# Rows of a group of four taken with a step of 4 instead of a step of 2

## The chip, the cores and the metric

The kernel is one program on one core of a Trainium2 chip. The metric is the time of one execution on the device in microseconds (us). The kernel before took 3278.6 us in the median of three runs (3276.79 to 3288.68 us). Its profile was taken of the run of 3288.68 us.

## The reference, cut to what matters

The network is two layers over eight sequences of 512 tokens with 128 features, each sublayer followed by a layer norm: attention, a feed-forward net, a second attention, and a mixture of experts. The change lies in the second attention. For each of 16 heads (64 wide) it computes:

```
q, k, v = x @ Wq, x @ Wk, x @ Wv            # k, v get 4 learned memory rows in front
dots = (l2norm(q) @ l2norm(k).T) * 10
dots = einsum('hg,bgij->bhij', W_pre_th, dots)     # the heads are mixed
dots = where(causal, dots, -max)                   # token i sees the memory and tokens 0..i
dots = where(dots < 64th largest of the row, -max, dots)
attn = einsum('hg,bgij->bhij', W_post_th, softmax(dots))   # mixed again
out  = (attn @ v) * head_scale * sigmoid(x @ Wg + bg);  out @ Wo
```

Each query row is mixed, cut to its 64 largest scores and normed by itself, so which rows are handled together is free.

## The kernel before, in words

The program has three phases: attention and feed-forward net of the first layer, the second attention, and the experts. The second (`second_phase`, line 703, with its body in `second_attention`) takes some 1.9 ms of the span.

**Tiles and units.** A sequence of 512 queries is cut into four tiles of 128 (`TILE_ORDER` = 3, 1, 2, 0). Scores of a tile are written head by head into `dots` (the profile calls it arena), with the query on the partition. Mixing heads needs heads on the partition, so a tile is worked in 16 units of 8 query rows by 16 heads = 128 partitions. One DMA on SyncE's queue (L909) gathers a unit from 8 partitions of `dots` into one of four `mixin` slots. Four units form a group of 32 rows (`GROUP`): all units of a group have the same width, up to the last column that any row of the group sees (`width`). Two units form a pair, and a step works on one pair; a sequence has 32 steps.

**Which rows.** `every(u)` (L833) says which 8 rows of a tile are unit u: a slice of 16 rows with a step of 2. So the first two units of a group share its first 16 rows, and the other two its last 16. The same function places a unit's 8 columns when the weights are turned back: ScalarE's copy into `at2` (L1261) writes 8 columns for each head and key block, 2 apart.

**The steps of a unit.** PE mixes (L1070) and adds a mask (L1072); ScalarE copies the result to `xs` (L1235); VectorE takes the maximum and moments; GpSimd and ScalarE (L1242, twice) find a threshold near the 64th score; VectorE picks the bound from it and writes the chosen weights with their sum (L1354 to L1394); GpSimd scales the second mixing matrix by the sum (L938); PE multiplies the weights with it, which turns them at the same time (`post`, L1083); ScalarE copies them to `at2` (L1261); and once a block of 64 queries is complete, PE multiplies it with the values (`values`, L1116).

**The tail.** Four memory rows stand in front of the keys, so the last 4 columns of a tile (tokens 124 to 127 of its own block) lie beyond its last full key block. `has_tail(s)` is true for a step whose rows can see them: before, only the last of a tile's 8 steps. There PE makes one more small product for each unit (`post_tail`, L1092, 4 columns as weights), ScalarE copies it to `tail` (L1266), and `values` adds its product (L1121) to the last 16 columns of the block.

**Order.** Every engine's order is written out by hand: a table of `put` calls (L788 to L805) lays the other work of the sequence (norms, keys, queries, scores, gates) into three slots A, B and C of each step. PSUM is four pairs of banks. Scores, keys, queries, gates and tails all go through the pair `banks_a` in one order of turns (`A_KEYS`, L862 to L869); PE may fill a bank when the copy two turns before has been read. VectorE and GpSimd wait for the tail's product before they write over the weights that it reads (L1389, L935).

Of the kernel before, what the change touches and what calls it, by code (L numbers as in the profile page):

```python
# [14 lines left out]
P = 128  # L15
# [5 lines left out]
UNSEEN = -2.0 ** 66  # L21
# [20 lines left out]
H1, HD1, MEM, TOPK = 16, 64, 4, 64  # L42
# [3 lines left out]
R8 = P // H1  # L46
SUBS = S // R8
PER_TILE = P // R8
GROUP = 4
RB = 64  # L50
# [4 lines left out]
SEQ = [PER_TILE * t + u for t in TILE_ORDER for half in ((0, 1) if t else (1, 0)) for u in range(PER_BLOCK * half, PER_BLOCK * (half + 1))]  # L55
PAIR = 2
# [20 lines left out]
def width(n):  # L77

    return MEM + GROUP * R8 * (n // GROUP + 1)
# [63 lines left out]
def scope(nc):  # L143

    ctx, sems = ExitStack(), []

    def sb(name, shape, dt=F32):
        return ctx.enter_context(nc.sbuf_tensor(name, shape, dt))

    def sem(name):  # L150
        s = ctx.enter_context(nc.semaphore(name))
        sems.append(s)
        return s

    return ctx, sb, sem, sems
# [547 lines left out]
def second_phase(nc, psum, d, x2_d, x3_d, dots, wts, x2_0):  # L703

    ctx, sb, sem, sems = scope(nc)
    with ctx:
# [7 lines left out]
        vx = sb("vx", [P, TT + 1, H1 * HD1])  # L714
# [1 line left out]
        sq = krow  # L716
        ssq, nrm = sb("ssq", [P, 2 * TT * H1]), sb("nrm", [P, 2, 2 * TT * H1])
        at2 = sb("at2", [P, TT, H1, RB])
        tail = sb("tail", [P, H1, PAIR * R8])
        gate, og = sb("gate", [P, NC, P]), sb("og", [P, NC, P])  # L720
        res = sb("res2", [P, TT, D])
        stats, mv, rstd = sb("stats2", [P, 6]), sb("mv2", [P, 2]), sb("rstd2", [P, 1])
# [52 lines left out]
        def second_attention(block, nb, first, full):  # L775
# [45 lines left out]
            def unit(m):  # L821
                return m // SUBS, SEQ[m % SUBS]

            def pair_of(s):
                return [(z, PAIR * s + z, SEQ[(PAIR * s + z) % SUBS]) for z in range(PAIR)]
# [5 lines left out]
                return m % SUBS // PER_TILE  # L831

            def every(u):  # L833
                at = PAIR * R8 * (u // PAIR)
                return slice(at + u % PAIR, at + PAIR * R8, PAIR)

            def last_piece(n):
                return len(pieces(width(n))) - 1
# [3 lines left out]
                return k < A_SLOTS or SEQ[k] // PER_TILE != SEQ[k - A_SLOTS] // PER_TILE or width(SEQ[k]) < width(SEQ[k - A_SLOTS])  # L842

            def has_tail(s):
                return SEQ[PAIR * s % SUBS] % PER_TILE == PER_TILE - PAIR

            def banks_of(what):
                if what[0] in ("xT", "g"):
# [131 lines left out]
            def _(pe):  # L980
# [6 lines left out]
                def d_bank(key):  # L987
                    if DV.nth(key) > 2:
                        pe.wait_ge(d_free, DV.nth(key) - 2)
                    return banks_d[DV.bank(key)]  # L990
# [105 lines left out]
                def values(r, second):  # L1096

                    b, n = unit(PER_BLOCK * r)
                    t, odd = divmod(n // PER_BLOCK, 2)
                    if second:  # L1100
                        bank = banks_d[DV.bank(("av", r))]
                    else:
                        pe.wait_ge(t_free, T.nth(PER_BLOCK * r + PER_BLOCK - 1))
                        if odd:
                            pe.wait_ge(a_free, A.nth(("tail", STEPS_BLOCK * (r + 1) - 1)))
                            pe.wait_ge(a_free, A.nth(("vx", b, TT, 1)))
                        if r % BLOCKS == 0:
                            pe.wait_ge(a_free, A.nth(("vx", b, TT - 1, 1)))
                            pe.wait_ge(memv_in, 16 * (b + 1))
                        bank = d_bank(("av", r))  # L1110
                    for c in range(NC // 2 * second, NC // 2 * (second + 1)):
                        col = RB * c
                        for k in range(t + 1):
                            for h in (2 * c, 2 * c + 1):
                                at = HD1 * (h % 2)
                                ins = nc.tensor.matmul(bank[at:at + HD1, col:col + RB], vx[:, k, HD1 * h:HD1 * h + HD1], at2[:, k, h, :],  # L1116
                                                       start=k == 0, stop=k == t and not odd)
                        if odd:
                            for h in (2 * c, 2 * c + 1):
                                at = HD1 * (h % 2)  # L1120
                                ins = nc.tensor.matmul(bank[at:at + HD1, col + RB - PAIR * R8:col + RB], vx[:, t + 1, HD1 * h:HD1 * h + HD1],  # L1121
                                                       tail[:, h, :], start=False, stop=True)
                    if second:
                        ins.then_inc(d_full, 1)
# [35 lines left out]
            def _(act):  # L1160

                def filled(key):
                    act.wait_ge(a_full, A.nth(key))
                    return banks_a[A.bank(key)]
# [89 lines left out]
                def posted(s):  # L1254
                    r = s // STEPS_BLOCK
                    if s % STEPS_BLOCK == 0 and r:
                        act.wait_ge(d_full, DV.nth(("av", r - 1)))
                    for z, m, n in pair_of(s):
                        t, u = n // PER_TILE, n % PER_BLOCK
                        act.wait_ge(t_full, T.nth(m))  # L1260
                        nc.scalar.copy(at2[:, 0:t + 1, :, every(u)],  # L1261
                                       banks_t[T.bank(m)][:, 0:P * (t + 1)].rearrange("p (k h i) -> p k h i", k=t + 1, h=H1)).then_inc(t_free, 1)
                    if has_tail(s):
                        bank = filled(("tail", s))
                        for z, m, n in pair_of(s):
                            ins = nc.scalar.copy(tail[0:MEM, :, every(n % PAIR)],  # L1266
                                                 bank[0:MEM, P * z:P * z + P].rearrange("p (h i) -> p h i", h=H1))
                        ins.then_inc(a_free, 1)

# [579 lines left out]
def network(nc, d, x2_d, x3_d, parts_d, maxes_d, gates_d, out_d):  # L1849
    with ExitStack() as ctx:  # L1850
        psum = {k: [ctx.enter_context(nc.psum_tensor(f"p{k}{i}", [P, 512], F32)) for i in range(2)] for k in "aomt"}
        arena = ctx.enter_context(nc.sbuf_tensor("arena", [P, SCORES_N], F32))
        wts2 = ctx.enter_context(nc.sbuf_tensor("wts2", [P, W2_N], F32))
        x2_0 = ctx.enter_context(nc.sbuf_tensor("x2s0", [P, TT, D], F32))
        first_phase(nc, psum, d, x2_d, parts_d, maxes_d, arena, wts2, x2_0)
        second_phase(nc, psum, d, x2_d, x3_d, arena, wts2, x2_0)
        third_phase(nc, psum, d, x3_d, gates_d, out_d, arena)


def constants():  # L1860

    f = np.float32
    half = HD0 // 2
    inv = (1.0 / f(10000.0) ** (np.arange(half, dtype=f) / f(half))).astype(f)
    freqs = np.arange(S, dtype=f)[:, None] * inv[None, :]
    d = np.arange(P) % HD0
    cos, sin = np.cos(freqs)[:, d % half].T, np.sin(freqs)[:, d % half].T
    sin = np.where((d < half)[:, None], -sin, sin)
    q = np.arange(P)
    sums = q[:, None] == q[None, :] // SUM_COLS * SUM_COLS + HD0 + q[None, :] % HD0  # L1870
    heads = (q[:, None] // HD1 == q[None, :] // HD1)
    dpre = (q[:, None] // H1 == q[None, :] // H1)
    dpost = (q[:, None] // H1 == q[None, :] % R8)
    rank = np.broadcast_to((TOPK - 1 - np.arange(WINDOW)) * TAKEN, (P, WINDOW))
    mask_s = np.where(q[None, :] > q[:, None], LOW, 0.0)
    mix = [np.where(np.arange(GROUP * R8)[None, :] > PAIR * (R8 * (v // PAIR) + q[:, None] // H1) + v % PAIR, UNSEEN, 0.0) for v in range(GROUP)]
    return dict(first=[cos, sin, np.eye(P), sums], masks=[np.eye(P), mask_s, mask_s.T],
                second=[np.eye(P), *thresholds(), rank], mix=[np.eye(P)] + mix, heads=heads, dpre=dpre, dpost=dpost,
                ident=np.eye(P))


def thresholds():


    first, slope = np.zeros((P, SUBS), np.float32), np.zeros((P, SUBS), np.float32)

    def quantile(share):

        lo, hi = -10.0, 10.0
        for _ in range(60):  # L1890
            mid = (lo + hi) / 2
            lo, hi = (mid, hi) if (1 + erf(mid / sqrt(2))) / 2 < share else (lo, mid)
        return lo

    for n in range(NARROW_FROM, SUBS):
        for q in range(P):
            seen = PAIR * R8 * (n // PAIR) + PAIR * (q // H1) + n % PAIR + 1 + MEM
            first[q, n] = quantile(1 - (AIM + 0.5) / seen)
            slope[q, n] = -1 / (2 * seen * exp(-first[q, n] ** 2 / 2) / sqrt(2 * pi))
        summed = sqrt(width(n) - GROUP * R8)  # L1900
        first[:, n], slope[:, n] = first[:, n] / summed, slope[:, n] / summed
    return first, slope


def laid_out(a):
# [3 lines left out]
    wq, wk, wv = qkv[:D], qkv[D:2 * D], qkv[2 * D:]  # L1909
    swap = (np.arange(D) // HD0) * HD0 + (np.arange(D) + HD0 // 2) % HD0  # L1910
    c = constants()

    def cols(v):
# [48 lines left out]
```

## Time and profile before

| | |
|---|---|
| median of 3 runs | 3278.6 us |
| the profiled execution | 3288.68 us |
| its span from the first to the last instruction | 3286.9 us |
| mean granted clock of TensorE | 0.911 |
| PE, VectorE, ScalarE, GpSimd busy | 2715.9, 2309.8, 2086.8, 1239.6 us |
| transfers from `arena` to `mixin` | 512, of 18 to 258 KB |
| copies into `at2` | 512, 198.4 us |
| copies into `tail` | 64, 13.2 us |

An engine's busy time says how much work it has, not whether it sets the end: for that the stretches and the waits are read. Steps are 32 to a sequence, and the pattern of one sequence returns eight times.

### The profile page before, as it was taken

To read this page: it belongs to the slowest core of one execution; us is meant where nothing else is said; L and a number is where in the kernel's file an instruction comes from. 1 tells how busy PE (TensorE), PEld (TensorE's weight loads), DVE (VectorE), ACT (ScalarE), POOL (GpSimd) and SP (SyncE) were. 2 spreads that over 40 slices of the span, in tenths; PEclk is the share of its full clock that TensorE was granted. 3 is DMA by queue.
4 is the path that set the end of the run, shared out by engine and by line. 5 is a ranking of instruction groups with operands and counts; after the bars stand their busy time and mean duration, and the time that the engine had idled before them with its cause. 6 is when DMAs were issued, how large, how long until landed. Compare 5 with 4: busy or idle time off the path is not lost. (4 is left out here: it accounts for less than half of the span.)

```text
span 3286.9 us, 59887 instructions
## 1 busy us (share of the span) xinstructions
PE 2715.9 (83%) x18884; PEld 1634.5 (50%) x18884; DVE 2309.8 (70%) x7740; ACT 2086.8 (63%) x5457; POOL 1239.6 (38%) x3658
## 2 busy tenths in 40 slices
PE   3678888888888888888888888888888888876898
PEld 1234333333333456555555555556556556555565
DVE  3445355444423399899799799899799888887465
ACT  0244655555453588788788788787787787874331
POOL 2111011101000256555565565565565565674000
PEclk6678889989889799999899999999999999987899
DMA  2111011001010211211211211211211211221342
GB/s 91 34 36 37 8 37 40 23 19 40 5 45 10 46 32 37 54 33 36 52 37 32 53 39 31 57 36 28 60 37 25 59 39 24 57 47 40 92 98 65
DMA packets 111295, 137.13 MB, mean 42 GB/s; under 512 B 20448, under 2 KB 90592, under 8 KB 110464
## 3 DMA queue, kind: packets, MB, share of 16 engines
q1 hardware_dynamic: 110976, 133.25, 17.8%
q8 instruction: 155, 2.54, 0.3%
q14 instruction: 164, 1.34, 0.1%
HBM read 47.62 MB, written 13.24 MB: 19 GB/s over the span
## 5 line engine op out<-in xcount | busy, mean ns | idle before, releaser
L1242 ACT ACTIVATE junk<-xs,thr 128x420 bf16<-128x420 f32 (+12 forms) x832 | 466.0, 570 | 74.8 <-POOL thr L957 59.8
L1083 PE MATMUL pt<-wsc,attn 128*128 128x128 f32 x2560 | 364.1, 292 | 101.9 <-POOL wsc L938 65.4
L1070 PE MATMUL pm<-mixin,pre_b 128*128 128x258 f32 (+15 forms) x1088 | 371.2, 457 | 91.2 <-ACT xs L1235 80.9
L1083 PEld LDWEIGHTS pt<-wsc,attn 128*128 128x128 f32 x2560 | 325.9, 200 | 192.7 <-POOL wsc L938 132.8
L615 DVE TENSOR_REDUCE row_max<-po 128x1 f32<-128x384 f32 (+3 forms) x352 | 209.5, 637 | 290.8 <-PE po L457 289.8
L1364 DVE MAX8 best<-left 128x8 f32<-128x420 f32 (+12 forms) x832 | 368.4, 483 | 0.0
L1036 PE MATMUL pa<-kT,qT 64*128 64x258 f32 (+3 forms) x1280 | 290.7, 457 | 85.6 <-ACT arena L1204 62.2
L1204 ACT ACTIVATE arena<-pa,nrm 128x258 f32<-128x258 f32 (+3 forms) x640 | 273.4, 477 | 105.1 <-PE pa L1036 99.4
L1394 DVE SCALAR_TENSOR_TENSOR attn<-xs,bound,ex 128x420 f32<-128x420 f32 (+14 forms) x480 | 226.6, 500 | 124.8 <-issue 62.0
L1070 PEld LDWEIGHTS pm<-mixin,pre_b 128*128 128x128 f32 x1088 | 179.9, 203 | 228.3 <-issue 198.0
L1261 ACT COPY at<-pt 128x128 f32<-128x128 f32 (+3 forms) x512 | 198.4, 450 | 114.7 <-PE po L1121 97.2
L1251 ACT ACTIVATE ex<-xs,negm 128x228 f32<-128x228 f32 (+15 forms) x512 | 239.5, 520 | 0.1
L381 POOL CAST parts<-rot 128x512 bf16<-128x512 f32 x16 | 9.8, 614 | 596.6 <-DVE rot L609 452.6
L938 POOL TENSOR_SCALAR wsc<-post_b,rsum 128x128 f32<-128x128 f32 x512 | 221.2, 443 | 26.3
L1036 PEld LDWEIGHTS pa<-kT,qT 64*128 64x128 f32 x1280 | 138.3, 198 | 176.2 <-ACT arena L1204 96.9
L1116 PE MATMUL po<-at,vx 128*64 128x64 f32 x5120 | 213.6, 235 | 0.4 <-ACT at L1261 0.4
L1302 DVE BATCH_NORM_STATS2 moments<-xs 128x6 f32<-128x388 f32 (+12 forms) x416 | 172.4, 454 | 55.8 <-ACT xs L1235 54.2
L931 POOL TENSOR_TENSOR rsum<-ssum,powers 128x2 f32<-128x2 f32 x256 | 186.7, 729 | 63.7 <-DVE attn L1394 45.0
L1116 PEld LDWEIGHTS po<-at,vx 128*64 128x64 f32 x5120 | 188.4, 146 | 22.9 <-issue 13.1
L1368 DVE MATCH_REPLACE8 left<-best,left 128x420 f32<-128x420 f32 (+12 forms) x416 | 196.0, 478 | 0.0
L1235 ACT COPY xs<-pm 128x258 f32<-128x258 f32 (+15 forms) x544 | 178.3, 379 | 25.5 <-PE pm L1072 12.7
L1306 DVE TENSOR_REDUCE negm<-xs 128x2 f32<-128x840 f32 (+15 forms) x256 | 182.4, 712 | 13.9 <-ACT xs L1235 13.5
(235 smaller groups left out, 5960.8 us busy)
## 6 DMA issues: line engine op xcount, KB each, us to landing
spread<-gates_dram SPq DMA_DIRECT2D x32, 512.0 KB, 7.9
mixin<-arena SPq DMA_DIRECT2D x32, 258.0 KB
mixin<-arena SPq DMA_DIRECT2D x32, 242.0 KB
mixin<-arena SPq DMA_DIRECT2D x32, 226.0 KB
mixin<-arena SPq DMA_DIRECT2D x32, 210.0 KB
mixin<-arena SPq DMA_DIRECT2D x32, 194.0 KB
parts_dram<-parts SPq DMA_DIRECT2D x16, 384.0 KB, 3.9
q_stack<-parts_dram SPq DMA_DIRECT2D x96, 64.0 KB
```

The lines of the kernel that those rows point to most:

```text
L615: nc.vector.tensor_reduce(row_max[:, i, h + odd:h + odd + 2 * n - 1:2], scores, X, ALU.max).then_inc(o_free, 1)
L938: nc.gpsimd.tensor_scalar(wsc[:, m % A_SLOTS], post_b[:, :], rsum[:, p, z:z + 1], 1.0, ALU.mult, ALU.mult).then_inc(attn_done, 1)
L1036: nc.tensor.matmul(a_bank(("qk", b, t, 2 * c + odd, z))[:, 0:jn], qT[at:at + HD1, c, P * t:P * t + P], kT[at:at + HD1, c, j0:j0 + jn], sta ...
L1070: ins = nc.tensor.matmul(bank[:, 0:jn], pre_b[:, :], mixin[:, m % MIX_SLOTS, j0:j0 + jn], start=True, stop=not last)
L1083: ins = nc.tensor.matmul(bank[:, P * k:P * k + P], attn[:, m % A_SLOTS, P * k:P * k + P], wsc[:, m % A_SLOTS], start=True, stop=True)
L1116: ins = nc.tensor.matmul(bank[at:at + HD1, col:col + RB], vx[:, k, HD1 * h:HD1 * h + HD1], at2[:, k, h, :], start=k == 0, stop=k == t and ...
L1204: nc.scalar.activation(dots[:, at:at + jn], filled(("qk", b, t, g, z))[:, 0:jn], ACT.Copy, scale=nrm[:, b % 2, col:col + 1]).then_inc(a_fr ...
L1242: ins = nc.scalar.activation(junk[:, z, 0:width(n)], xs[:, m % X_SLOTS, 0:width(n)], ACT.Sign, scale=-1.0, bias=thr[:, s % LIVE, z:z + 1], ...
L1251: nc.scalar.activation(ex[:, m % E1_SLOTS, 0:width(n)], xs[:, m % X_SLOTS, 0:width(n)], ACT.Exp, bias=negm[:, s % LIVE, z:z + 1]).then_inc ...
L1261: nc.scalar.copy(at2[:, 0:t + 1, :, every(u)], banks_t[T.bank(m)][:, 0:P * (t + 1)].rearrange("p (k h i) -> p k h i", k=t + 1, h=H1)).then ...
L1364: done[z] = chain.mark(nc.vector.max(out=best[:, z, 8 * k:8 * k + 8], in_=left[:, z, 0:wn]))
L1394: ins = nc.vector.scalar_tensor_tensor(out=attn[:, m % A_SLOTS, 0:wn], in0=xs[:, m % X_SLOTS, 0:wn], scalar=bounds[z], in1=ex[:, m % E1_SL ...
```

## The change

Rows are taken with a step of 4 out of all 32 rows of a group, instead of a step of 2 out of 16. With it the mask and the table of first thresholds follow the rows, `tail` is twice as wide, and the last two steps of a tile have a tail instead of the last one, since each of the four units now holds rows of the group's end.

```diff
-        tail = sb("tail", [P, H1, PAIR * R8])
+        tail = sb("tail", [P, H1, GROUP * R8])
             def every(u):
-                at = PAIR * R8 * (u // PAIR)
-                return slice(at + u % PAIR, at + PAIR * R8, PAIR)
+                at = GROUP * R8 * (u // GROUP)
+                return slice(at + u % GROUP, at + GROUP * R8, GROUP)
             def has_tail(s):
-                return SEQ[PAIR * s % SUBS] % PER_TILE == PER_TILE - PAIR
+                return SEQ[PAIR * s % SUBS] % PER_TILE >= PER_TILE - GROUP
 # values:
-   ins = nc.tensor.matmul(bank[at:at + HD1, col + RB - PAIR * R8:col + RB], vx[:, t + 1, HD1 * h:HD1 * h + HD1],
+   ins = nc.tensor.matmul(bank[at:at + HD1, col + RB - GROUP * R8:col + RB], vx[:, t + 1, HD1 * h:HD1 * h + HD1],
 # posted:
-   ins = nc.scalar.copy(tail[0:MEM, :, every(n % PAIR)],
+   ins = nc.scalar.copy(tail[0:MEM, :, every(n % GROUP)],
 # constants:
-    mix = [np.where(np.arange(GROUP * R8)[None, :] > PAIR * (R8 * (v // PAIR) + q[:, None] // H1) + v % PAIR, UNSEEN, 0.0) for v in range(GROUP)]
+    mix = [np.where(np.arange(GROUP * R8)[None, :] > GROUP * (q[:, None] // H1) + v, UNSEEN, 0.0) for v in range(GROUP)]
 # thresholds:
-            seen = PAIR * R8 * (n // PAIR) + PAIR * (q // H1) + n % PAIR + 1 + MEM
+            seen = GROUP * R8 * (n // GROUP) + GROUP * (q // H1) + n % GROUP + 1 + MEM
```

On PE, at the end of tile 1 (first sequence), the product for a new tail (L1092) comes in between a product of the next sequence's scores (L1036) and its key rows (L1009):

```order
 L1083 MATMUL pt<-wsc,attn 128x128 x4
 L1036 MATMUL pa<-kT,qT 128x132 x2
+L1092 MATMUL pa<-wsc,attn 4x128 x2
 L1009 MATMUL po<-wts,xe 128x512 x2
 L1070 MATMUL pm<-mixin,pre_b 128x324
```

Nothing else moved there: two products were added, one for each unit of the pair. The same stands once in each of the four tiles.

On ScalarE, at the same place one step later, the copy of a tail (L1266) comes in behind the copy of the weights (L1261):

```order
 L1242 ACTIVATE junk,signs<-xs,thr 128x292 x2
 L1261 COPY at<-pt 128x32x8 x2
+L1266 COPY tail<-pa 4x128 x2
 L1183 COPY qT<-pa 128x512 x2
 L1242 ACTIVATE junk,signs<-xs,thr 128x292 x2
```

Two copies are added there, again once in each tile.

On PE, in the product with the values at the end of tile 1, the tail's products are 32 columns wide instead of 16:

```order
 L1116 MATMUL po<-at,vx 64x64 x4
-L1121 MATMUL po<-tail,vx 64x16 x2
-L1116 MATMUL po<-at,vx 64x64 x4
-L1121 MATMUL po<-tail,vx 64x16 x2
+L1121 MATMUL po<-tail,vx 64x32 x2
+L1116 MATMUL po<-at,vx 64x64 x4
+L1121 MATMUL po<-tail,vx 64x32 x2
```

Their number and place stay. VectorE and SyncE have the same instructions in the same order as before; GpSimd differs in the size of one memset of `tail`.

## Rows read from the trace of the kernel before

**Rows 1.** The page's first lines: span, busy time of each engine

```profile
span 3286.9 us, 59887 instructions
PE 2715.9 (83%) x18884; PEld 1634.5 (50%) x18884; DVE 2309.8 (70%) x7740; ACT 2086.8 (63%) x5457; POOL 1239.6 (38%) x3658
```

**Rows 2.** Stretches: length, busy us (instructions) by engine, PE clock, DMA share, GB/s

```profile
1598.00:1843.00 245.00, 210.83 (x1712) 144.27 (x1711) 214.79 (x814) 192.28 (x570) 142.11 (x442) 0.94 0.19 40
1606.00:1686.00 80.00, 65.64 (x462) 42.67 (x461) 76.75 (x239) 66.21 (x176) 47.32 (x143) 0.94 0.19 42
1686.00:1702.00 16.00, 15.69 (x204) 10.75 (x204) 11.37 (x49) 10.88 (x34) 8.97 (x32) 1.00 0.17 35
...
1814.00:1850.00 36.00, 32.08 (x320) 24.34 (x320) 18.77 (x112) 21.35 (x83) 17.52 (x54) 0.86 0.26 60
```

**Rows 3.** ScalarE's groups: line, operation, shape, count | busy us, mean ns | idle before

```profile
L1261 ACT COPY at<-pt 128x512 f32<-128x512 f32 x128 | 69.7, 601 | 5.5 <-PE po L1116 5.5
...
L1261 ACT COPY at<-pt 128x128 f32<-128x128 f32 x128 | 29.2, 292 | 72.5 <-PE po L1121 69.4 <-PE pt L1083 3.1
...
L1266 ACT COPY tail<-pa 4x128 f32<-4x128 f32 x64 | 13.2, 257 | 0.0
```

**Rows 4.** PE in order of time: start us, us, what, count [idle before]

```profile
1691.77 0.25 PE L1121 MATMUL po<-tail,vx 128*64 128x16 f32 x4
1691.86 0.66 PE L1116 MATMUL po<-at,vx 128*64 128x64 f32 x16
1692.36 0.25 PE L1121 MATMUL po<-tail,vx 128*64 128x16 f32 x4
...
1809.22 0.60 PE L1092 MATMUL pa<-wsc,attn 128*4 128x128 f32 x4
1809.75 0.41 PE L1070 MATMUL pm<-mixin,pre_b 128*128 128x36 f32 x2
```

**Rows 5.** Who waited for the old tails: us in total, times

```profile
  ACT at L1261: 97.2, 32
  PEld pa L1036: 13.5, 13
  PE pa L1036: 6.7, 13
```

**Rows 6.** Stretches as in rows 2: loads at the start, then mixin transfers

```profile
5.00:25.00 20.00, 6.61 (x8) 2.43 (x8) 6.78 (x7) 0.00 (x0) 13.13 (x11) 0.85 0.53 213
1600.00:1612.00 12.00, 9.96 (x39) 5.17 (x38) 9.41 (x31) 10.51 (x33) 7.69 (x27) 0.86 0.48 105
```

**Rows 7.** What PE's instructions on mixin waited for: us in total, times

```profile
  DMA mixin<-arena: 27.5, 29
```

**Rows 8.** PE in order of time, first and fourth sequence: waits for mixin

```profile
1109.97 1.77 PE L1070 MATMUL pm<-mixin,pre_b 128*128 128x420 f32 x2 [4.68 <-DMA mixin<-arena]
...
1112.18 1.77 PE L1070 MATMUL pm<-mixin,pre_b 128*128 128x420 f32 x2 [0.42 <-DMA mixin<-arena]
...
1840.54 0.97 PE L1070 MATMUL pm<-mixin,pre_b 128*128 128x420 f32 x2 [0.58 <-DMA mixin<-arena]
```

**Rows 9.** In order of time, end of tile 1 of the third sequence: PE, ScalarE, VectorE

```profile
1738.97 0.81 PE L1036 MATMUL pa<-kT,qT 64*128 64x132 f32 x4
1739.71 3.55 PE L1009 MATMUL po<-wts,xe 128*128 128x512 f32 x4
...
1739.81 0.63 ACT L1204 ACTIVATE arena<-pa,nrm 128x132 f32<-128x132 f32 x2 [0.28 <-PE pa L1036]
...
1745.47 0.59 ACT L1183 COPY qT<-pa 128x512 f32<-128x512 f32 x1 [2.78 <-PE pa L1023]
...
1748.53 0.14 DVE L1393 MEMSET attn<- 128x96 f32 x1 [0.58 <-DVE picked L1372]
```

**Rows 10.** In order of time, end of tile 3 of the same sequence: ScalarE, VectorE

```profile
1683.38 0.43 ACT L1242 ACTIVATE junk<-xs,thr 128x164 bf16<-128x164 f32 x1 [1.10 <-POOL thr L957]
...
1686.18 1.08 ACT L1261 COPY at<-pt 128x512 f32<-128x512 f32 x2
...
1698.21 0.66 ACT L1261 COPY at<-pt 128x256 f32<-128x256 f32 x2 [1.62 <-PE po L1121]
...
1702.02 0.42 DVE L1394 SCALAR_TENSOR_TENSOR attn<-xs,bound,ex 128x196 f32<-128x196 f32 x1 [3.66 <-issue]
```

**Rows 11.** The same, end of tile 2 and start of tile 0: ScalarE

```profile
1809.83 0.40 ACT L1242 ACTIVATE junk<-xs,thr 128x132 bf16<-128x132 f32 x1 [1.56 <-POOL thr L949]
...
1824.75 0.43 ACT L1261 COPY at<-pt 128x128 f32<-128x128 f32 x2 [6.58 <-PE po L1121]
```

## The prediction

> **What bounds the kernel now.** I read the page's busy times first. No engine is full over the span: PE 83%, VectorE 70%, ScalarE 63% [rows 1]. The average mixes phases, so I cut the second attention, the only phase that the change touches, into stretches. In one sequence (1598 to 1843 us) VectorE is busy 214.8 of 245 us, PE 210.8 and ScalarE 192.3. Inside a wide tile (1606 to 1686 us) VectorE is busy 76.8 of 80 us and ScalarE 66.2: VectorE sets the pace, and ScalarE has 14 us of room. Where tiles change it is otherwise: from 1686 to 1702 us PE is busy 15.7 of 16 us and VectorE 11.4, and from 1814 to 1850 us VectorE is busy only 18.8 of 36 us [rows 2]. There a chain through PE and ScalarE is the path: ScalarE stands until the products with the values are done (97.2 us in 32 waits, [rows 5]), then copies the weights, then makes the exponentials for which VectorE stands (3.66 us at 1702 us, [rows 10]). So an edit counts where tiles change and is mostly hidden inside them. VectorE has the same instructions as before, so what bounds the wide stretches does not move.
>
> **The added tails.** 32 steps more have a tail (8 sequences x 4 tiles). Each adds two copies on ScalarE; 64 old ones took 13.2 us [rows 3], so 32 new pairs add 13.2 us of work. On PE each adds four instructions that hold it 0.53 us (1809.22 to 1809.75 us, [rows 4]), 17 us in all. What of it lies on the path is read at the four places:
> - Tile 3: where the new copy goes, ScalarE has just stood 1.10 us for a threshold [rows 10]. Hidden.
> - Tile 2: ScalarE stands 1.56 us one step later [rows 11]. Hidden.
> - Tile 1: PE's new product goes in front of the key rows at 1739.71 us, and needs a bank of the pair whose copy ScalarE starts only at 1739.81 us; behind it are queued the key rows and the queries, for which ScalarE stands 2.78 us, and VectorE stands 0.58 us for the exponentials behind those [rows 9]. PE is late by its 0.53 us plus some 0.4 us for the bank: 0.9 us, and VectorE's wait grows by about 0.6 us. 8 x 0.6 = 5 us.
> - Tile 0: PE has no idle time, but soon after it stands 0.58 us for a transfer to mixin [rows 8], which takes up the 0.53 us. 8 x 0.1 = 1 us.
>
> Sum 6 us. The ends are 0 and 37 us: nothing exposed, or all of PE's 17 us and once more the 20.2 us that PE stood for old tails [rows 5].
>
> **The wider tail products.** 1024 instructions go from 16 to 32 columns. Four of 16 columns hold PE 0.09 us (22 ns each), sixteen of 64 columns 0.50 us (31 ns each) [rows 4]. 32 columns should lie a third of the way: 3 ns more, 3 us in all, of which I take 2 us on the path. The ends are 0 and 9 us (the full 9 ns for each).
>
> **The transfers to mixin.** They read 8 partitions, now spread over 32 instead of 16. In a stretch full of them the queue moved 105 GB/s at a DMA share of 0.48 of 16 engines, that is 13.7 GB/s for each busy engine. The loads at the start moved 213 GB/s at 0.53, 25 GB/s for each [rows 6]. So a mixin transfer runs at about half of what an engine can do, and something that two engines share is likely to hold it. The page "SBUF — State Buffer" of the Trainium skill (section "Door 1: The DMA port swizzle") says that four neighbouring partitions share a port, so that 16 partitions reach 4 ports and 32 reach 8; by that rule the reading side would double, and the rate in this trace agrees with a halved one. But PE stands for these transfers only 27.5 us in 29 waits, counted on both its rows [rows 7]: once 4.68 us in the first sequence, which holds other delays too, and then about half a microsecond at the fourth wide unit of each sequence (0.42 and 0.58 us, [rows 8]). I take 1.1 us at the start (half a first transfer) and 8 x 0.5 us, together 5 us of gain; the ends are 0 and 27.5 us. The writing side is unchanged and may hold the rate as it is.
>
> **The copies into at2.** 512 copies write columns 4 apart instead of 2. Now they take 292 ns for 128 columns and 601 ns for 512 [rows 3]: 309 ns over 384 columns, 0.80 ns a column, so a step of 2 looks free of charge. A step of 4 stands in no row. Below, the cost is nothing (a smaller one has no reason: the columns are as many). Above, I bound it by each column costing a second 0.80 ns: 128 copies of each width of 128, 256, 384 and 512 columns are 163,840 columns, 131 us more on ScalarE. I take nothing, since the rate up to now follows the number of columns alone; the other end is a rival.
>
> **Sum.** 6 + 2 - 5 + 0 = +3 us against the profiled execution's own 3288.7 us. That one was the slowest of the three, 10.1 us above the median, and no edit depends on that; so 3278.6 + 3 = 3282 us. Mask, thresholds and memset are of the same count and place, and a row's threshold depends on the row alone, so the search finds the same.
>
> **Rivals.**
> - The copies' step costs (slower). For it: nothing in the rows excludes it. Inside a wide tile ScalarE would go from 66.2 to about 73 of 80 us (8 steps x 0.82 us), still under VectorE's 76.8, so it stays hidden. Where tiles change it is exposed: at 3 to 1 two copies of 512 (0.82 us, 1686.18 us) and two of 256 (0.41 us, 1698.21 us) ahead of the exponentials that VectorE stands for [rows 10]; at 2 to 0 two of 384 (0.61 us) and two of 128 (0.20 us, 1824.75 us, [rows 11]); in tile 0 and after it some five pairs of 128, 1.0 us. 3.0 us a sequence, 24 us, with the 3 us above 3306 us. It decides from a cost of about 0.45 ns a column (13 us exposed). The page "Advanced Engine Details and Errata" (section "SBUF Cachelines") of the Trainium skill says that SBUF is read in lines of 16 bytes and wants two hits on a line for full pace: a step of 2 gives two, a step of 4 one. No row here shows which holds for writes.
> - The transfers give back more. If a halved transfer frees all 27.5 us [rows 7] and the tails cost 6: 3278.6 - 27.5 + 8 = 3259 us. Against it: most of that is one wait at the start.
> - The transfers do not get faster, because the writing side holds them: 3282 + 5 = 3287 us. The change then does not do to the DMA what the rows suggest.
> - The tails' turns of the bank pair cost as the old ones did: half of the upper end of 37 us, about 20, plus 2 and 1: 3302 us. For it: 13 of 32 old tails made PE stand [rows 5].
>
> **How the numbers follow.** The forecast 42% (own range 3271 to 3294), costly copies 28%, transfers giving back more 15%, transfers as before 9%, costly turns 6%. What this kernel's measurement can tell from no change is about 0.5%, 16 us. Faster: 15 and 1 of the forecast's own spread, 16%. Same: 40 of the forecast, 7 of unchanged transfers, 3 of copies with half a price, 50%. Slower: 25 + 6 + 3 = 34%. The range for 8 in 10 goes from inside the faster case, 3262 us, to beyond the costly copies, 3314 us.
>
> **What would show it.** The copies into at2: 292 and 601 ns again, or up to 395 and 1010 ns. The tail group: 128 copies, 26 us, and who waits for them. The DMA share in the stretch behind a tile change: the same bytes at the same share (13.7 GB/s an engine), or a share that falls; PE's waits for mixin below 27.5 us. VectorE's stretch inside wide tiles still at 96%, and its wait behind tile 3 still 3.66 us or 1.2 us longer. The prediction is wrong if the copies' mean goes up by more than 100 ns, or if PE's time behind tile changes shrinks by more than the waits for transfers held.

## The result, and the profile after

| | before | after |
|---|---|---|
| median | 3278.8 us | 3336.2 us (3330.0 to 3339.0) |
| ratio | | 1.0167, 95% interval [1.0141, 1.0193] |
| profiled execution | 3288.7 us | 3324.3 us |

The change costs some 55 us. The forecast was 3282 us with a range up to 3314 us: the time lies outside it, on the slow side. The two profiled executions, which all rows of before and after come from, lie only 36 us apart: the one of before is the slowest of its four, the one of after the fastest of its five. One execution of e1 (5130 us) and one of before beside it (4320 us) ran in a slower state and count in no ratio or median below.

The first lines of the page answer to [rows 1]: span, then busy time by engine.

```profile
span 3322.4 us, 60231 instructions
PE 2737.8 (82%) x19012; PEld 1644.5 (49%) x19012; DVE 2312.3 (70%) x7740; ACT 2211.2 (67%) x5521; POOL 1238.4 (37%) x3658
```

Only ScalarE has much more to do: 2211.2 us instead of 2086.8. VectorE's work is what it was, so the lost time is waiting. ScalarE's groups answer to [rows 3] (columns as there):

```profile
L1261 ACT COPY at<-pt 128x512 f32<-128x512 f32 x128 | 126.5, 1096 | 5.6 <-PE po L1116 5.6
L1261 ACT COPY at<-pt 128x384 f32<-128x384 f32 x128 | 97.9, 878 | 22.2 <-PE po L1121 14.6 <-PE po L1116 5.4 <-PE pt L1083 2.3
L1261 ACT COPY at<-pt 128x256 f32<-128x256 f32 x128 | 67.6, 640 | 13.9 <-PE po L1121 13.1 <-PE po L1116 0.8
L1266 ACT COPY tail<-pa 4x128 f32<-4x128 f32 x128 | 42.0, 427 | 0.1
L1261 ACT COPY at<-pt 128x128 f32<-128x128 f32 x128 | 39.9, 423 | 62.3 <-PE po L1121 59.6 <-PE pt L1083 2.7
```

A copy of 512 columns takes 1096 ns instead of 601, one of 128 takes 423 instead of 292. The slope is (1096 - 423)/384 = 1.75 ns a column instead of 0.80. All 512 copies hold ScalarE 332.0 us instead of 198.4. The tail's copies slow down too, from 257 to 427 ns each.

Who waited for the tail (us in total, times) answers to [rows 5]:

```profile
  ACT at L1261: 87.2, 32
  PEld pa L1036: 27.4, 22
  PE pa L1036: 17.2, 21
```

PE now stands 17.2 us for a bank that holds a tail, after 6.7 us. And the waits for mixin [rows 7], with the page's line on the queue that carries nearly all transfers (packets, MB, share of 16 engines; it was 17.8% before):

```profile
  DMA mixin<-arena: 10.9, 6
...
q1 hardware_dynamic: 110976, 133.25, 14.7%
```

The transfers did get faster: the same bytes at a smaller share, and 29 waits became 6. The second attention as one stretch (columns as in [rows 2]), of before:

```profile
1146.00:3030.00 1884.00, 1585.68 (x13396) 1104.37 (x13394) 1677.48 (x6426) 1487.84 (x4435) 1120.08 (x3484) 0.95 0.19 41
```

and of after:

```profile
1146.00:3030.00 1884.00, 1576.93 (x13209) 1087.94 (x13209) 1651.43 (x6270) 1587.05 (x4414) 1096.43 (x3420) 0.95 0.13 40
```

The share fell from 0.19 to 0.13 at nearly the same rate, while ScalarE is busy 99 us more in the same 1884 us and VectorE gets through less.

**Where the time went.** VectorE takes the maximum of a step's rows (L1306) once a step, so its starts mark the steps. I took each step's length as the median over the eight sequences, before and after. 21 of 32 steps agree within 0.15 us. The others, and step 3, which moves in e1, in us, after minus before (steps counted from 0 in a sequence):

| where | steps | after | copies alone (e1) | tails alone (e3) |
|---|---|---|---|---|
| inside tile 3 | 3, 5, 6 | +2.1 | +3.3 | +0.3 |
| tile 3 to 1 | 11 | +1.0 | +0.8 | 0 |
| inside tile 1 | 16 | +0.2 | +0.2 | 0 |
| tile 1 to 2 | 19, 20 | +1.4 | -0.7 | +0.9 |
| inside tile 2 | 24 | +0.5 | +0.5 | 0 |
| tile 2 to 0 | 27, 28 | +1.3 | +3.0 | +0.9 |
| tile 0 and on | 30, 0 | -0.2 | 0 | +0.2 |
| sum of all 32, times 8 | | +55 | +59 | +17 |

The sum of the medians is not the whole: from the first of these starts to the last, the profiled executions differ by 43, 57 and 19 us, since some steps are long in a few sequences only. That after's +55 is also the measured difference is chance.

The largest single step, inside tile 3, is one where nothing was expected. PE's rows there (start us, us, what, count, [idle before]), of before:

```profile
1636.50 1.88 PE L1044 MATMUL pa<-wts,xe 128*128 128x512 f32 x4
1638.97 1.16 PE L1051 MATMUL pa<-xe,wts 128*128 128x128 f32 x8 [0.59 <-ACT vx L1210]
1641.78 1.11 PE L1070 MATMUL pm<-mixin,pre_b 128*128 128x258 f32 x4 [1.65 <-ACT xs L1235]
```

and of after, with VectorE's wait behind it:

```profile
1640.22 1.88 PE L1044 MATMUL pa<-wts,xe 128*128 128x512 f32 x4
1643.02 1.16 PE L1051 MATMUL pa<-xe,wts 128*128 128x128 f32 x8 [0.92 <-ACT vx L1210]
1645.83 2.06 PE L1070 MATMUL pm<-mixin,pre_b 128*128 128x258 f32 x4 [1.65 <-ACT xs L1235]
...
1648.35 0.67 DVE L1302 BATCH_NORM_STATS2 moments<-xs 128x6 f32<-128x484 f32 x1 [1.70 <-ACT xs L1235]
```

ScalarE's longer copies into at2 sit ahead of its copies of `vx`, so PE waits 0.92 us for a bank instead of 0.59. Then the same four mixing products take 2.06 us instead of 1.11. The reason is in the stretches (length, busy us by engine, PE clock, DMA share, GB/s); of before:

```profile
1634.50:1641.50 7.00, 4.90 (x28) 3.43 (x28) 6.96 (x22) 6.18 (x16) 3.45 (x12) 1.00 0.01 3
1641.50:1645.50 4.00, 3.72 (x25) 3.34 (x26) 3.16 (x7) 3.34 (x10) 2.22 (x8) 1.00 0.10 21
```

and of after:

```profile
1638.00:1645.50 7.50, 4.95 (x28) 3.48 (x28) 7.46 (x23) 6.67 (x17) 3.58 (x12) 1.00 0.00 0
1645.50:1649.50 4.00, 3.67 (x15) 3.15 (x16) 1.86 (x5) 2.38 (x7) 1.64 (x4) 0.57 0.04 14
```

From the start of the product at L1044 to that of the mixing products PE needed 5.61 instead of 5.28 us (1640.22 to 1645.83, 1636.50 to 1641.78), and its granted clock behind that was 0.57 instead of 1.00, near the lower level of 1.2 GHz. In the 4 us around these mixing products it was 0.57, 1.00, 1.00, 1.00, 0.59, 1.00, 0.59, 1.00 in the eight sequences before, and 0.57 to 0.59 in all eight after.

The delay is there without the clock too. In e1 this step (the sixth of a sequence, step 5) ran at 1.00 in four sequences and took 11.2 us, in before 9.3 us in four at 1.00 (10.0 in a fifth). VectorE's waits in it, fourth sequence, of before:

```profile
1886.89 0.67 DVE L1302 BATCH_NORM_STATS2 moments<-xs 128x6 f32<-128x484 f32 x1 [0.19 <-ACT xs L1235]
```

and of e1 (its line numbers are 4 higher):

```profile
1906.36 0.67 DVE L1306 BATCH_NORM_STATS2 moments<-xs 128x6 f32<-128x484 f32 x1 [1.29 <-ACT xs L1239]
1907.76 0.67 DVE L1306 BATCH_NORM_STATS2 moments<-xs 128x6 f32<-128x484 f32 x1 [0.74 <-ACT xs L1239]
```

2.03 us instead of 0.19 us: that is nearly all of the step's 1.9 us.

Other rows of the table are mostly clock. Step 28, at the change from tile 2 to tile 0, as stretches (columns as in [rows 2]): of before, third and fourth sequence,

```profile
1817.57:1827.50 9.93, 9.18 (x133) 8.44 (x131) 3.88 (x27) 3.35 (x18) 2.96 (x11) 0.64 0.04 9
2058.61:2064.44 5.83, 5.08 (x101) 4.38 (x97) 3.89 (x26) 3.34 (x18) 2.95 (x11) 1.00 0.08 16
```

of e1, third, and of e3, fourth:

```profile
1835.27:1845.14 9.87, 9.07 (x133) 8.33 (x131) 3.88 (x27) 3.39 (x18) 2.95 (x11) 0.66 0.04 9
2069.72:2075.58 5.86, 5.12 (x101) 4.39 (x97) 3.89 (x27) 3.35 (x18) 2.95 (x11) 1.00 0.07 15
```

At a like clock the step takes what it did, with costly copies and with two tails. Step 3 is the same: 9.6 to 9.8 us at 0.73 to 0.75 in e1's second to seventh sequences and also in one of before (9.6 at 0.73), 8.5 us at 0.87 and above.

The change from tile 3 to tile 1 went as the rival with costly copies had it. ScalarE, answering to [rows 10]:

```profile
1686.66 1.96 ACT L1261 COPY at<-pt 128x512 f32<-128x512 f32 x2
...
1691.64 1.89 ACT L1261 COPY at<-pt 128x512 f32<-128x512 f32 x2
1693.34 0.65 ACT L1266 COPY tail<-pa 4x128 f32<-4x128 f32 x2
```

and VectorE there: its two waits for exponentials, which in before were 0.99 us and 3.66 us:

```profile
1698.85 0.14 DVE L1393 MEMSET attn<- 128x96 f32 x1 [1.97 <-issue]
...
1708.49 0.42 DVE L1394 SCALAR_TENSOR_TENSOR attn<-xs,bound,ex 128x196 f32<-128x196 f32 x1 [3.69 <-issue]
```

The first wait grew by 1.0 us, because 0.8 us of the pair of 512 and 0.24 us of the tail pair lie ahead of those exponentials. The second did not grow, though the two copies of 256 ahead of it went from 0.66 to 1.05 us: VectorE was by then behind by the same 1 us.

### The profile page after: what moved, and what is told of

Same layout as the page of the kernel before. It is cut to its first block and busy times, and to the rows that moved or that the text cites. A ratio compares the mean times of both kernels' runs of the same rounds, so it can differ in the third digit from the quotient of the medians.

```text
span 3322.4 us, 60231 instructions
## 1 busy us (share of the span) xinstructions
PE 2737.8 (82%) x19012; PEld 1644.5 (49%) x19012; DVE 2312.3 (70%) x7740; ACT 2211.2 (67%) x5521; POOL 1238.4 (37%) x3658
## 5 line engine op out<-in xcount | busy, mean ns | idle before, releaser
L1261 ACT COPY at<-pt 128x128 f32<-128x128 f32 (+3 forms) x512 | 332.0, 759 | 104.0 <-PE po L1121 87.2
L1036 PE MATMUL pa<-kT,qT 64*128 64x258 f32 (+3 forms) x1280 | 301.8, 466 | 99.8 <-ACT arena L1204 64.7
L1204 ACT ACTIVATE arena<-pa,nrm 128x258 f32<-128x258 f32 (+3 forms) x640 | 273.0, 477 | 98.1 <-PE pa L1036 96.0
L1036 PEld LDWEIGHTS pa<-kT,qT 64*128 64x128 f32 x1280 | 143.1, 203 | 196.4 <-ACT arena L1204 102.4
L955 POOL TENSOR_SCALAR shift<-signs 128x2 f32<-128x2 f32 x416 | 90.9, 218 | 278.1 <-ACT junk L1242 263.1
```

What stands on the lines that cost most here:

```text
L1036: nc.tensor.matmul(a_bank(("qk", b, t, 2 * c + odd, z))[:, 0:jn], qT[at:at + HD1, c, P * t:P * t + P], kT[at:at + HD1, c, j0:j0 + jn], sta ...
L1204: nc.scalar.activation(dots[:, at:at + jn], filled(("qk", b, t, g, z))[:, 0:jn], ACT.Copy, scale=nrm[:, b % 2, col:col + 1]).then_inc(a_fr ...
L1261: nc.scalar.copy(at2[:, 0:t + 1, :, every(u)], banks_t[T.bank(m)][:, 0:P * (t + 1)].rearrange("p (k h i) -> p k h i", k=t + 1, h=H1)).then ...
```

## The experiments

In short, with the ratio to before in the same session. The last column, the difference to before at the same granted clock, is worked out below.

| run | what | ratio [95%] | at the same clock |
|---|---|---|---|
| after | all of the change | 1.0167 [1.0141, 1.0193] | +41 us |
| e1 | at2 copies with step 4 | 1.0160 [1.0133, 1.0186] | +29 us |
| e2 | DMA source rows | 1.0014 [0.9995, 1.0033] | -6 us |
| e3 | two tails a tile | 1.0069 [1.0052, 1.0086] | +15 us |
| e4 | after, written with step 2 | 1.0063 [1.0047, 1.0078] | +10 us |
| e5 | at2 copies with step 1 | one run, 3274.9 us | -3 us |
| e6 | at2 copies with step 8 | 1.0177 [1.0148, 1.0206] | +32 us |
| e7 | source rows, queries permuted | 1.0055 [1.0039, 1.0072] | -7 us |
| e8 | e3, PE's tail product later | 1.0023 [1.0008, 1.0038] | +4 us |
| e9 | one copy for a pair | 1.0008 [0.9990, 1.0025] | 0 us |
| e10 | after, one copy for a pair | 1.0084 [1.0065, 1.0102] | +10 us |
| e11 | wide tail products | 1.0021 [1.0003, 1.0038] | 0 us |
| e12 | after with its costs mended | 0.9997 [0.9982, 1.0013] | -5 us |

### The copies alone: e1

```diff
+            def placed(u):
+                at = GROUP * R8 * (u // GROUP)
+                return slice(at + u % GROUP, at + GROUP * R8, GROUP)
-   nc.scalar.copy(at2[:, 0:t + 1, :, every(u)],
+   nc.scalar.copy(at2[:, 0:t + 1, :, placed(u)],
```

> The kernel before with one edit: ScalarE's copy into at2 writes its 8 columns 4 apart instead of 2 (the rows of the output then stand in another order than the reference's). Theory 1, the step of the write costs: the copies take 420 to 430 ns at 128 columns and about 1100 ns at 512, as in the changed kernel, and the time goes up by 35 to 55 us, most of the measured 57. Theory 2, the second tail and its turns of the bank pair cost: the copies may be slower, but VectorE sets the pace and hides them; within 10 us of before.

Measured: 3331.3 us, 1.6% or 52 us slower by the ratio. Its ScalarE groups:

```profile
L1265 ACT COPY at<-pt 128x512 f32<-128x512 f32 x128 | 127.0, 1103 | 7.2 <-PE po L1120 7.2
...
L1265 ACT COPY at<-pt 128x128 f32<-128x128 f32 x128 | 39.7, 418 | 80.2 <-PE po L1125 77.4 <-PE pt L1087 2.7
```

The step of the written columns alone gives the whole price of the copies and, alone, nearly the whole slowdown. Part of that is clock, as e1's mean of 0.903 against 0.913 shows.

### The source rows alone: e2

```diff
-   tile = dots[every(u), SCORES_AT[t]:SCORES_AT[t] + H1 * wt]...
+   tile = dots[placed(u), SCORES_AT[t]:SCORES_AT[t] + H1 * wt]...
```

> The kernel before with one edit: the transfer to mixin reads 8 partitions 4 apart instead of 2 (so it computes with other rows than its mask says). Both theories: transfers faster by about a third, waits of PE for mixin from 27.5 to about 11 us, time lower by 0 to 16 us. A theory 3, that the other rows at the source cost time by contention, would have it above before.

Measured: 3287.2 us against 3282.3, not the 0 to 16 us less that was expected. The queue and PE's waits:

```profile
  DMA mixin<-arena: 11.0, 6
...
q1 hardware_dynamic: 110976, 133.25, 14.9%
```

All of the relief in the transfers is here, and no gain in the plain time. The gain is in the steps all the same: step 0, where the fourth wide unit is mixed, takes 5.8 to 6.1 us instead of 6.3 to 6.9 in the second to eighth sequences, 6.9 us over all eight. The same execution gives back 7.3 us in steps 1 to 6, where more sequences run at a lower clock: step 3 took 9.7 us or more at 0.71 to 0.77 in four sequences, in before 9.6 us in one. At the same clock e2 is 6 us faster than before. Whether the other source rows bring the lower clock with them is open; in e7, with the same source rows, the steps do the same.

### The tails alone: e3

```diff
-   return SEQ[PAIR * s % SUBS] % PER_TILE == PER_TILE - PAIR
+   return SEQ[PAIR * s % SUBS] % PER_TILE >= PER_TILE - GROUP
```

(and `tail` and its products 32 wide, as in the change)

> The kernel before with the last two steps of each tile given a tail, and the tail's products 32 columns wide; rows and steps as before. Theory 1: 3 to 12 us more (my sum had 8). Theory 2: 35 us or more, with PE waiting for tail copies 45 us instead of 20.

Measured: 3306.0 us, 23 us more, which neither theory had. Who waited for the tail hardly moved against [rows 5], so the turns behind a tail are not the price:

```profile
  ACT at L1261: 95.4, 32
  PEld pa L1036: 14.7, 14
  PE pa L1036: 7.5, 14
```

But the new products themselves wait for a bank until ScalarE has read it at L1204, which no tail's product did in before, and all that is queued behind them waits too:

```profile
PE pa L1092 <- ACT arena L1204: 7.7, 15, 1.1
```

What grew besides are VectorE's waits for products that PE has queued behind the tail: for the output projection (L1131) from 6.0 us in 4 waits to 13.0 us in 10, for the key rows (L1009) from 9.1 us in 7 to 14.9 us in 20:

```profile
DVE krow L1420 <- PE po L1009: 14.9, 20, 4.7
DVE res L1437 <- PE po L1131: 13.0, 10, 3.9
```

In tile 0 of the third sequence the new product makes this wait (none stood there before):

```profile
1838.58 0.29 DVE L1437 TENSOR_TENSOR res<-po,x2s 128x128 f32<-128x128 f32 x1 [0.76 <-PE po L1131]
```

### After, but written as before: e4

The changed kernel, with `placed(u)` as `every(u)` was before in the copies into at2 and tail:

```diff
+                at = PAIR * R8 * (u // PAIR)
+                return slice(at + u % PAIR, at + PAIR * R8, PAIR)
```

> The changed kernel with one edit: the copies into at2 and tail write columns 2 apart again (the rows of the output then stand in another order). Theory 1: the copies are back at 292 and 601 ns, and the time is within 12 us of the kernel before, on either side. Theory 2: it stays 35 us or more above the kernel before.

Measured: 3301.3 us, 1.0063, as e3, and above the 12 us that were allowed for it. So the change's cost is the step of the writes (1.7% down to 0.6%) plus the tails. At the same clock e4's +10 us is what e3 and e2 give together (15 - 6), so nothing else of it shows.

### Other steps: e5 and e6

```diff
+   return slice(R8 * u, R8 * u + R8)      # e5: 8 columns in a row
+   return slice(u, RB, R8)                # e6: 8 columns apart
```

> The kernel before with the copies into at2 written with a step of 1 (the rows of the output then stand in another order). If a step of up to two columns is free: 292 and 601 ns again, time as before. If every step costs: shorter copies, below 500 ns at 512 columns.

> The kernel before with the copies into at2 written with a step of 8 (rows in another order). If what counts is one write for each 16 bytes, a step of 8 costs what a step of 4 does: 423 and 1096 ns, 1.6% slower. If the cost grows with the distance: clearly more than 1.75 ns a column, and more than 2% slower.

Measured for e5, 3274.9 us in its one run:

```profile
L1264 ACT COPY at<-pt 128x512 f32<-128x512 f32 x128 | 67.9, 583 | 5.6 <-PE po L1119 5.6
...
L1264 ACT COPY at<-pt 128x128 f32<-128x128 f32 x128 | 28.8, 286 | 66.9 <-PE po L1124 63.9 <-PE pt L1086 3.1
```

and for e6, 3339.0 us:

```profile
L1264 ACT COPY at<-pt 128x512 f32<-128x512 f32 x128 | 129.7, 1124 | 5.5 <-PE po L1119 5.5
...
L1264 ACT COPY at<-pt 128x128 f32<-128x128 f32 x128 | 40.9, 432 | 76.6 <-PE po L1124 74.0 <-PE pt L1086 2.6
```

The slopes are 0.77 ns a column at step 1, 0.80 at 2, 1.75 to 1.78 at 4, 1.80 at 8. It is a threshold between 8 and 16 bytes, not a cost that grows with the distance. The page "Advanced Engine Details and Errata" (section "SBUF Cachelines") of the Trainium skill speaks of lines of 16 bytes that want two hits; by that rule steps 1 and 2 are at full pace and 4 and 8 alike pay, and these rows agree, for ScalarE's writes of 4-byte values.

### The tail's product later on PE: e8

e3 with the product put behind the key rows and the projection of its step:

```diff
-   if 3 <= s < N + 3 and has_tail(s - 3):
-       post_tail(s - 3)
    for what in beside.get(s, []):
        (key_rows if what[0] == "rows" else project)(*what[1:])
+   if 3 <= s < N + 3 and has_tail(s - 3):
+       post_tail(s - 3)
```

> The kernel before with two tails (as in e3), and on PE the tail's product put behind the key rows and the output projection of its step instead of ahead of them. If the tails cost by standing ahead of products that VectorE waits for: the steps 19 and 30 of a sequence, 0.6 and 0.8 us longer in e3, are back, and the time is 5 to 15 us below e3. If they cost by their turns of the bank pair or their copies: as e3.

Measured: 3291.0 us, 15 us below e3 (11 us at the same clock). The two waits are back near their old size, at the price of a wait of ScalarE:

```profile
DVE krow L1420 <- PE po L1009: 8.2, 5, 4.7
DVE res L1437 <- PE po L1131: 7.9, 5, 3.9
...
ACT tail L1266 <- PE pa L1092: 6.0, 10, 1.1
```

Step 19 is back to its length in before; step 30 is still 0.5 us longer (0.8 in e3). The wait of the tail's own products for a bank that ScalarE reads at L1204 shrinks as well, from 7.7 us to 2.5 us, and the one for a bank that it reads at L1183, 7.7 us in before and in e3, is gone from PE's row. So e8 shows the place of the product to be the price, but not how much of it is the queue behind it and how much its own wait for a bank.

### One copy for both units: e9 and e10

e9 is before, e10 is after. Both units of a pair are copied by one instruction that reads their two PSUM banks in turn (the two banks are declared as one tensor `both`; lines shortened):

```diff
-   for z, m, n in pair_of(s):
-       nc.scalar.copy(at2[:, 0:t + 1, :, every(u)], banks_t[T.bank(m)]...
+   nc.scalar.copy(at2[:, 0:t + 1, :, R8 * u:R8 * (u + PAIR)]...         # e9
+   nc.scalar.copy(at2[:, 0:t + 1, :, own:own + GROUP * R8]...[:, :, :, at:at + PAIR],   # e10
+                  psum["both"][:, :, 0:P * (t + 1)].rearrange("p z (n i) -> p n i z", i=R8))
```

> The kernel before with one copy into at2 for both units of a pair: its innermost step alternates between the two banks of PSUM, and it writes 16 columns in a row. Reads from two banks in turn stand in no row so far. If they cost nothing: 0.80 ns a column and 256 fixed parts of 190 ns less, some 49 us less on ScalarE, 0 to 15 us faster in all. If they cost like a write with a step of 4: 130 us more on ScalarE less 49, 20 to 40 us slower.

> The changed kernel with one copy into at2 for both units of a pair instead of two: it reads the two PSUM banks in turn and so writes two neighbouring columns out of each four. Theory (what costs is a write that is the only one in its 16 bytes): 0.80 ns a column again, 384 ns for 256 columns to about 1010 ns for 1024, ScalarE 150 us less than in the changed kernel, time as the two tails alone cost, 3295 to 3310 us. Rival (any step that leaves 16 bytes half empty costs, or a jump of 12 bytes does): above 1.2 ns a column, time 3325 to 3340 us.

Measured for e9: 3286.7 us, no change; ScalarE's busy time falls by 15 us (2086.8 to 2071.8), not by 49. For e10: 3308.7 us, and its groups:

```profile
L1262 ACT COPY at<-pt 128x1024 f32<-128x1024 f32 x64 | 67.4, 1052 | 6.2 <-issue 6.2
...
L1262 ACT COPY at<-pt 128x256 f32<-128x256 f32 x64 | 25.1, 392 | 75.6 <-issue 44.2 <-PE po L1121 27.8 <-PE pt L1083 3.6
```

(1052 - 392)/768 = 0.86 ns a column, although it still leaves half of each 16 bytes untouched and jumps 12 bytes. So two writes in each 16 bytes are nearly enough (e9's full rows go at 0.81); the theory holds, and the time falls from after's 3336 to 3309 us. At the same clock that is +10 us, as e4.

### Wide products, and all mended: e11 and e12

e11 is before with the tail's products 32 columns wide and nothing else. e12 is e10 with e8's order and one copy for both tails.

> The kernel before with only the tail's products made 32 columns wide instead of 16 (1024 instructions; the same steps have a tail). Theory: 0 to 5 us more, 3279 to 3287 us, not to be told from before. Rival (part of what the two tails cost is the wider product): 3290 to 3300 us.

> The changed kernel with its three costs mended: one copy into at2 for both units (two neighbouring columns at a time), one copy into tail for both units, and PE's tail product put behind the key rows and projections of its step. Theory (writes alone in their 16 bytes and the place of the tail's product are all that the change cost): 3270 to 3292 us, within 0.5% of before. Rival (something else of the change costs, such as the tails' turns in the bank pair): 3300 us and above. A version faster than before by more than 0.5% is expected by neither.

Measured for e11: 3284.2 us, 1.0021 with an interval that begins at 1.0003; 1 to 12 us, and 0 at the same clock. For e12: 3279.2 us against 3278.2, the same as before. Every cost of the change is in those three edits' reach. At the same clock e12 is 5 us faster than before, near what the source rows give alone.

### Source rows without the costs: e7

```diff
+   nc.scalar.copy(xq[:, :].rearrange("p (g i v) -> p g i v", i=R8, v=GROUP), spread(bank[:, :]))
-   at = PAIR * R8 * (u // PAIR)
-   return slice(at + u % PAIR, at + PAIR * R8, PAIR)
+   at = GROUP * R8 * (u // GROUP)
+   return slice(at + u % GROUP, at + GROUP * R8, GROUP)
+   # placed(u), for at2 and tail: slice(R8 * u, R8 * u + R8)
```

(cut: the products with Wq read `xq`; mask and first thresholds follow the rows)

> The kernel before with the queries laid out in another order: one more copy on ScalarE in each sequence (128x512) puts query 8v+i of a group of 32 on partition 4i+v. So a unit's DMA reads 8 partitions 4 apart as in the changed kernel, while a unit holds 8 neighbouring queries: the copies write 8 columns in a row, and each tile has one step with a tail, as before. Theory (columns 2 apart already at full pace, transfers hidden anyway): copies into at2 at 0.77 to 0.80 ns a column (286 to 600 ns), mixin's wait below 27.5 us, time within 0.5% of before, 3275 to 3290 us. Rival (what the DMA gains is on the path once nothing else is in its way): 3255 to 3268 us.

Measured: 3294.2 us, 0.55% slower: neither theory. Its copies are as expected (584 and 284 ns), the medians of its steps sum to the same as before's within 0.2 us over the program, and its mean granted clocks are lower (0.900 to 0.907). At the same clock it is 7 us faster than before, and its step 0 is shorter by 0.8 us, as in e2: the rival's gain is there in part, and the lower clock takes more than it gives. Why the clock is lower stays open.

## Why the prediction was wrong

**The clock first.** The executions of before lie on a line: 62 of them, with clocks from 0.903 to 0.921, fit 2.4 us more for each 0.001 of granted clock less, and scatter 2.7 us about it. Taking each kernel's time against that line gives the last column of the table above. There the parts add up: 29 (copies) + 15 (tails) - 6 (source rows) = 38 us, where after has 41. In plain times they don't (52 + 23 + 5 = 80 us against 55): by the line the three parts lose 23, 8 and 11 us to the clock when they are alone (means 0.903, 0.909 and 0.908, before's is 0.913), and the whole change loses only 14 (0.909). This is a correlation over runs, good to some 3 us; e1, e6, e7 and e10 reach below the line's lowest clock, and a loss of clock that an edit brings about is part of its cost in plain time. That a longer wait on ScalarE's side comes before a lower clock was seen at one place, inside tile 3; the delay was isolated there (e1 at 1.00), but not the cause of the clock.

**The step that failed: the copies into at2, "I take nothing".** I had both ends right, nothing and a second 0.80 ns a column, and took the wrong one, "since the rate up to now follows the number of columns alone". A step of 2 that is free says nothing of a step of 4 if there is a threshold between, and the rows held no other step. The measured extra is 0.95 ns a column; ScalarE's copies are busy 133.6 us longer (the two of a pair overlap a little) against my upper 131. The page "Advanced Engine Details and Errata" (section "SBUF Cachelines") of the Trainium skill, which I cited with the rival, had the threshold, and the chance of 28% for the rival was too low.

**The rival with that price had the work right, the time half, and the places wrong.** It gave 24 us for the copies; e1 measures 52 [44, 61], and 29 at the same clock. It counted the tile changes (3.0 us a sequence) and held the inside of wide tiles for hidden, since ScalarE would be busy 73 of 80 us there. ScalarE is busy 71.4 of 80 us in after:

```profile
1607.00:1687.00 80.00, 64.15 (x451) 41.47 (x450) 74.99 (x223) 71.36 (x175) 47.04 (x140) 0.96 0.14 41
```

But room on average is not room at each step. Steps 3, 5 and 6 lie where the `vx` and gate banks turn and the mixed rows get too wide for one piece (516 columns in two of 258), and there the delay goes through ScalarE's order to PE and back: 3.3 us a sequence in e1, 26 us of its 52. Of the 3.3 us step 5 alone has 1.9 at clock 1.00, and step 3's 1.2 us is clock. At the tile changes e1's rows sum to 3.1 us (0.8 - 0.7 + 3.0), the rival's 3.0 as if it were right, but that is luck: most of the 3.0 at tile 2 to 0 is clock too, since step 28 takes 9.9 us at 0.66 in e1 and 9.9 us at 0.64 in before. That 24 is near the 29 us at the same clock is luck of the same kind.

**The tails: 6 + 2 us forecast, 23 us measured (e3), 15 at the same clock.** The sum of PE's work and the upper end of 37 us were fair. Tile 3: "hidden", and it was. Tile 1: 0.6 us forecast, 0.9 measured, at clock 1.00. Tile 2: "hidden"; the medians are 0.9 us longer, but the one sequence of e3 that ran both steps at 1.00 took 5.7 and 5.9 us, as before's did, so this is clock and the tail is hidden. Tile 0: 0.1 us forecast since a wait for mixin follows; step 30 grew by 0.8 us, because the output projection stands between PE's tail product and that wait, and VectorE waits for it, and step 0 of the next sequence gives back 0.6: 0.2 us are left. That is 1.1 us a sequence, 9 of the 15 us; the rest, and why the clock is lower with two tails, is open. What the sum lacked is the clock, and the new product's own wait for a bank beyond the 0.4 us at tile 1. The wider products, 2 us, hold within e11's interval. The rival on the turns of the bank pair named 3302 us, near e3, by the wrong cause: the wait for those turns went from 6.7 to 7.5 us only. It did grow in after, to 17.2 us, where the tail's copies are slower.

**The transfers: right mechanism, and a gain of about the right size, hidden by the clock.** PE's waits fell from 27.5 to 10.9 us as the reading side of the sum said. But the DMA share in the second attention fell by a third (0.19 to 0.13), not by half, so the reading side was not all that held them. In plain time e2 gives +5 us [-2, +11] where 5 us less were forecast. At the same clock it is -6 us, e7 -7 us, and step 0 is shorter by 6.9 us over the eight sequences of e2 and by 7.7 us in after: the waits were on the path there, and a lower clock in the steps behind took the gain.

**What held.** VectorE's work is unchanged (2309.8 and 2312.3 us), and so is its wait at 1702 us (3.66 and 3.69 us).

## What to carry to other kernels

A layout that is free at one step of a strided write may double in price at the next; if no row shows the new step, measure it or take the dearer end, and look for a change of regime where 4-byte values come to stand alone in 16 bytes. Before calling an engine's extra work hidden, follow it at the places where its order feeds another engine's bank, not in the average of a stretch: here tile 3 had 14 us of room for 7.1 us of extra work, and one step still grew by 1.9 us. And when a small product is put ahead of others on a busy engine, ask who waits for what is queued behind it; moving it behind them gave back 15 of 23 us. Compare a step's length at a like granted clock before giving it a cause.

## What the runs showed of the hardware that was not expected

- ScalarE writes 4-byte values at 0.77 and 0.80 ns a column for steps of 1 and 2, and at 1.75 to 1.80 ns for steps of 4 and 8. Two neighbouring columns out of each four go at 0.86 ns (e10).
- ScalarE reads two PSUM banks in turn, column by column, without a price a column: in e9, 1024 columns take 1004 ns and 256 take 384 ns, 0.81 ns a column.

```profile
L1261 ACT COPY at<-pt 128x1024 f32<-128x1024 f32 x64 | 64.2, 1004 | 6.2 <-issue 6.2
...
L1261 ACT COPY at<-pt 128x256 f32<-128x256 f32 x64 | 24.6, 384 | 69.9 <-issue 33.4 <-PE po L1121 33.0 <-PE pt L1083 3.6
```

- Whole executions of one kernel differ by their mean granted TensorE clock: 3261.9 us at 0.921 and 3293.8 us at 0.907 in one session. Small edits move that mean (0.909 after, 0.903 in e1, 0.904 in e7, 0.912 in e12), so a few tenths of a per cent can be clock and not the edit's own work. One step (28) took 5.8 us at 1.00 and 9.9 us at 0.64 in one execution of before.
- Spreading a transfer's 8 source partitions over 32 instead of 16 lowers the DMA share in the second attention from 0.19 to 0.13. The rule of the Trainium skill's page "SBUF — State Buffer" (section "Door 1: The DMA port swizzle"), by which 16 partitions reach half as many ports as 32, has the direction right; a halved time is not what the share shows.
